# Gate values taken out of the gathered rows, routed rows weighed by token in the attention

## What is computed

```python
xn = layernorm(x)                                  # 8192 x 128
# branch 1: linear attention, 16 heads of 8 channels, in chunks
r, k, v = proj(mix_r(xn)), proj(mix_k(xn)), proj(mix_v(xn))   # mix: xn and xn one token back
A = einsum(r, k) * Wmat                            # inside a chunk
y = A @ v + (r @ state) * wb                       # and from the state before it
state = ws * state + (k * wk).T @ v
s = y @ Wo.T + bo
# branch 2: mixture of experts
probs = softmax(xn @ gate_W.T)                     # 8 experts, the 2 best of each token
routed = sum over the 2 chosen e: probs[e] * (silu(xn @ w1[e]) * (xn @ w3[e])) @ w2[e]
shared = mean over 8 of (silu(xn @ w1s) * (xn @ w3s)) @ w2s
f = 0.5 * shared + 0.5 * routed
out = x + s * silu(f)
```

## Time and profile before

| | us |
|---|---|
| three runs | 879.22, 885.76, 897.25 |
| median | 885.76 |
| the profiled execution | 878.21 |
| its span | 876.4 |

### The profile page before, as it was taken

One profiled execution on the slowest core, in us unless ns is written; L12 is line 12 of the kernel. 1 busy time (PEld: TensorE's weight loads), 2 busy tenths in 40 slices (PEclk: granted clock), 3 DMA queues, 4 the chain that ended last, 5 costly groups with the idle time before them and its releaser, 6 DMA issues.

```text
span 876.4 us, 25917 instructions
## 1 busy us (share of the span) xinstructions
PE 729.4 (83%) x9696; PEld 582.4 (66%) x9696; DVE 585.2 (67%) x1253; ACT 471.9 (54%) x1000; POOL 445.1 (51%) x493
## 2 busy tenths in 40 slices
PE   3777989888788898788879888988889789999993
PEld 2566878766666777667657766766667666676762
DVE  6989988845455755545545455554554489999994
ACT  6755877645454555445545455554555545554551
POOL 2433312346556564555563555545554546666663
PEclk9999999988988989899999999999998899999997
DMA  9921123011111222322222222322232367777641
GB/s 246 227 85 37 41 83 50 14 39 39 38 33 44 78 83 74 112 72 84 77 81 61 87 82 81 114 68 83 82 75 67 110 195 218 214 225 218 194 148 49
DMA packets 106042, 87.83 MB, mean 100 GB/s; under 512 B 20611, under 2 KB 90885, under 8 KB 105925
## 3 DMA queue, kind: packets, MB, share of 16 engines
q1 hardware_dynamic: 96836, 66.96, 26.0%
q0 software_dynamic: 9088, 19.21, 8.6%
HBM read 51.40 MB, written 34.73 MB: 98 GB/s over the span
## 4 chain that ended last, share of the span: by engine, by line
PE 35%; DVE 28%; issue 15%; ACT 10%; another core or an unknown queue 8%; DMA 2%; POOL 1%; ACTq 0%; POOLq 0%; DVEq 0%; SPq 0%
DVE hidden L1099 8%; PE banks L1396 6%; PE banks L1397 5%; PE banks L1398 5%; DVE hidden L1202 4%; DVE wwords L1186 4%; ACT hidden L697 3%; PE banks L1435 3%; PE banks L1414 2%; PE banks L1415 2%; PE banks L1416 2%; PE banks L1530 2%; ACT hidden L702 2%; ACT ybuf L724 2%
## 5 line engine op out<-in xcount | busy, mean ns | idle before, releaser
L1099 DVE TENSOR_TENSOR hidden<-hidden,banks 128x512 f32<-128x512 f32 x206 | 140.7, 683 | 173.9 <-ACT hidden L697 139.7
L576 POOL DMA_INDIRECT srows<-normed_rows,source x142 | 143.9, 1013 | 128.2 <-DVE picked_gate L1080 83.1
L702 ACT CAST hidden<-hidden 128x512 f16<-128x512 f32 x206 | 127.2, 618 | 150.9 <-DVE hidden L1099 135.8
L585 POOL DMA_INDIRECT expert_rows<-ybuf,dest x142 | 144.0, 1014 | 119.7 <-ACT ybuf L724 88.8
L1396 PE MATMUL banks<-sxh,wwords 128*128 128x256 f16 x568 | 164.1, 289 | 27.9 <-issue 21.6
L1397 PE MATMUL banks<-sxl,wwords 128*128 128x256 f16 x568 | 164.3, 289 | 13.0 <-issue 12.8
L1105 DVE TENSOR_TENSOR hidden<-hidden 128x512 f16<-128x512 f32 x178 | 123.1, 692 | 77.3 <-ACT hidden L702 53.0
L1398 PE MATMUL banks<-sxh,wwords 128*128 128x256 f16 x568 | 164.4, 290 | 11.0 <-issue 10.9
L1414 PE MATMUL banks<-wwords,hidden 128*128 (+1 forms) x824 | 155.5, 227 | 12.2 <-issue 6.7
L1416 PE MATMUL banks<-wwords,hidden 128*128 (+1 forms) x824 | 152.7, 226 | 8.9 <-issue 8.9
L1415 PE MATMUL banks<-wwords,hidden 128*128 (+1 forms) x824 | 153.4, 226 | 5.0 <-issue 5.0
(11 more groups left out here) (188 smaller groups left out, 1572.8 us busy)
## 6 DMA issues: line engine op xcount, KB each, us to landing
rows<-x SPq DMA_DIRECT2D x32, 256.0 KB, 4.5
rows<-expert_rows SPq DMA_DIRECT2D x32, 256.0 KB, 3.4
normed_rows<-rows SPq DMA_DIRECT2D x16, 256.0 KB, 5.1
r_rows<-rows SPq DMA_DIRECT2D x32, 128.0 KB
rd_rows<-rows SPq DMA_DIRECT2D x32, 128.0 KB
stage<-r_rows SPq DMA_DIRECT2D x16, 256.0 KB, 4.6
k_rows<-rows SPq DMA_DIRECT2D x32, 128.0 KB
kd_rows<-rows SPq DMA_DIRECT2D x32, 128.0 KB
```

What stands on the lines that cost most here:

```text
L576: G.indirect_dma_start(srows[:, r % NXB, t, :], None, rows_in, bass.IndirectOffsetOnAxis(source[:, r * TPU + t:r * TPU + t + 1], 0)).then_ ...
L585: G.indirect_dma_start(rows_out, bass.IndirectOffsetOnAxis(dest[:, r * TPU + t:r * TPU + t + 1], 0), ybuf[:, r % NYB, t, :], None).then_in ...
L702: A.copy(guh[:, v % 2, h * 2 * UNIT:(h + 1) * 2 * UNIT], gu[:, i % 2, :]).then_inc(sem["gu_hi"], 1)
L1099: V.tensor_tensor(gu[:, i % 2, :], sg[:, i % 2, :], psum[2 * (i % 2) + 1][:, :], ALU.mult).then_inc(sem["gated"], 1)
```

## The change

Gate values no longer travel with the rows. `rows_in` has 128 numbers a row (512 bytes), and the write of the probabilities (`sp_probs`), VectorE's picking of gate values and the expert flags it used are gone. ScalarE copies a routed unit's output unweighted, in one 128x256 operation. The gate value of each token's first and second expert is kept by token: 1/z and exp(second - first)/z, in `zsum` and `pick`, which a second small Exp on ScalarE and a 128x64 product on VectorE make. In the attention ScalarE multiplies the two routed rows of each token by them (`act_weigh`, four 128x128 operations for each of k = 0 and 1) before Pool adds them.

The lists of the attention are put in another order. ScalarE: both weighings of a unit stand around the copy of the state product, and the masks of the next unit are done before the second cast of y. Pool: both additions of a unit stand together, behind the mask of a unit two ahead, and before the last addition of the unit before. SP: the loads of decayed r and k and of the routed rows come ahead of x and of the store.

```diff
-    RW = P + EXPERTS
-    rows_in = nc.dram_tensor("normed_rows", (NTOK, RW), F32, kind="Internal").ap()
+    rows_in = nc.dram_tensor("normed_rows", (NTOK, P), F32, kind="Internal").ap()
...
+        gates = [zsum, pick]
...
-            def sp_probs():
-                nc.sync.wait_ge(sem["gates"], 1)
-                nc.sync.dma_start(rows_in[:, P:RW].rearrange("(t p) e -> p t e", p=P), probs[:, :, :]).then_inc(sem["probs_out"], 16)
...
-            sp_x(0)
-            for u in range(NA + 2):
-                if u >= 2:
-                    sp_end(u - 2)
+            sp_rd(2)
+            for u in range(NA + 1):
+                if u >= 1 and u + 2 < NA:
+                    sp_rd(u + 2)
                 if u + 2 < NA:
                     sp_moe(u + 2)
-                if u + 1 < NA:
-                    sp_x(u + 1)
+                if u + KRING < NA:
+                    sp_kd(u + KRING)
+                if u < NA:
+                    sp_x(u)
+                if u > 0:
+                    sp_end(u - 1)
                 if u + RRING < NA:
                     sp_r(u + RRING)
-                if u + 2 < NA:
-                    sp_rd(u + 2)
                 if u + KRING < NA:
-                    sp_kd(u + KRING)
                     sp_k(u + KRING)
...
             def pool_sorted(r):
...
-                    G.wait_ge(sem["probs_out"], 16)
...
-                    G.wait_ge(sem["gate_picked"], r - NXB + 1)
...
             def pool_add(u, step):
...
-                    G.wait_ge(sem[f"picked{u % PRING}"], 32 * (u // PRING + 1))
+                    G.wait_ge(sem["weighed0"], u + 1)
+                    G.wait_ge(sem["weighed1"], u + 1)
...
             for u in range(-2, NA + 3):
-                if at(u + 1):
-                    pool_add(u + 1, 1)
+                if at(u - 1):
+                    pool_low(2 * (u - 1))
+                    pool_low(2 * (u - 1) + 1)
                 if at(u + 2):
                     pool_mask(2 * (u + 2))
                 if at(u):
-                    pool_end(u)
-                if at(u + 2):
-                    pool_add(u + 2, 0)
-                    pool_mask(2 * (u + 2) + 1)
+                    pool_add(u, 0)
+                    pool_add(u, 1)
+                if at(u - 1):
+                    pool_end(u - 1)
                 if at(u + 1):
-                    pool_low(2 * (u + 1))
-                    pool_low(2 * (u + 1) + 1)
+                    pool_mask(2 * (u + 1) + 1)
...
             def act_route():
-                A.wait_ge(sem["route"], 7)
+                A.wait_ge(sem["route"], ROUTE_CHOSEN)
                 A.activation(ta[:, :, :], ta[:, :, :], ACT.Exp, scale=1.0 / SW).then_inc(sem["exps"], 1)
+                A.activation(top[1][:, :], top[1][:, :], ACT.Exp, scale=1.0 / SW).then_inc(sem["exps"], 1)
...
-                    for t in range(TPU):
-                        i = A.mul(ybuf[:, r % NYB, t, :], src[:, t * P:(t + 1) * P], slot_gate[:, r % GRING, t:t + 1])
-                    i.then_inc(sem["y_out"], 1)
+                    A.copy(ybuf[:, r % NYB, :, :].rearrange("p t d -> p (t d)"), src).then_inc(sem["y_out"], 1)
...
+            def act_weigh(u, k):
+                A.wait_ge(sem[f"picked{u % PRING}"], 32 * (u // PRING + 1))
+                if u == 0:
+                    A.wait_ge(sem["gates"], 2)
+                for b in range(4):
+                    at = tile(u, b)
+                    i = A.mul(picked[k][:, u % PRING, b, :], picked[k][:, u % PRING, b, :], gates[k][:, at:at + 1])
+                i.then_inc(sem[f"weighed{k}"], 1)
...
             for u in range(-2, NA + 3):
-                if at(u):
-                    act_mask(u, 0)
-                    act_mask(u, 1)
-                if at(u - 2):
-                    act_moe(u - 2)
-                    act_high(2 * (u - 2) + 1)
-                if at(u):
-                    act_mask(u, 2)
-                    act_mask(u, 3)
                 if at(u - 1):
-                    act_inter(u - 1)
+                    act_weigh(u - 1, 0)
                 if at(u):
                     act_kv(u, 0)
                     act_kv(u, 1)
                 if at(u - 1):
                     act_high(2 * (u - 1))
+                if at(u + 1):
+                    act_mask(u + 1, 2)
+                    act_mask(u + 1, 3)
+                if at(u - 1):
+                    act_moe(u - 1)
+                if at(u + 1):
+                    act_mask(u + 1, 0)
+                    act_mask(u + 1, 1)
+                if at(u - 1):
+                    act_high(2 * (u - 1) + 1)
+                if at(u):
+                    act_weigh(u, 1)
+                    act_inter(u)
...
-                V.memset(eun[:, :, 0:1], 1.0).then_inc(sem["unit_step"], 1)
...
-                V.tensor_tensor(eun[:, :, 0:EXPERTS - 1], eun[:, :, 0:EXPERTS - 1], eun[:, :, 1:EXPERTS],
-                                ALU.subtract).then_inc(sem["unit_experts"], 1)
...
-                V.tensor_tensor(probs[:, :, :], ta[:, :, :], rep(zsum[:, :], EXPERTS), ALU.mult).then_inc(sem["gates"], 1)
+                V.tensor_tensor(pick[:, :], top[1][:, :], zsum[:, :], ALU.mult).then_inc(sem["gates"], 1)
```

39 lines of the change are left out of this document (8 added, 31 removed).

## The result

The changed kernel took 841.22 us (median of 4 runs, 838.31 to 843.32), beside 885.2 us (879.22 to 897.25) for the kernel before: 0.952 of it, 95% interval 0.946 to 0.958. Its profiled execution took 841.8 us with a span of 840.0 us, 36.4 us less than before. I had forecast 880 us and a range of 862 to 898, so the size was wrong, and with it the forecast of no change that can be measured.

What follows compares the result with a forecast made beforehand. TensorE, losing 136 us beside Pool's indirect transfers, bounds the routed stage; VectorE runs gapless in the attention's middle units. -0.95 - 0.9 = -1.85 us gave 876.4 us profiled, 883.9 on the median's scale; predicted 880, range 862 to 898.

Steps and rivals of the forecast that it cites:

- Gathers: Routed stage: Pool waits only for the transpose, gather starts about 1 us earlier, row 6% shorter; taken as 0.
- the routed stretch moving by over 10 us: Sign, routed stage: the prediction is wrong if the stretch with gathers moves by over 10 us.
- ScalarE in the routed units: Routed stage: one copy for two multiplications saves 0.25 us per unit, hidden from TensorE; 0, bounds 0 and -17 us.
- rival C: Routed stage: shorter eviction shows through Pool's burst, up to 0.25 us per typical unit, -5 to -17 us; chance 0.15.
- Rival B: Routed stage: shorter rows shrink the transfers' drag on TensorE, a quarter -17, all -68 us, 808 to 859; chance 0.08.
- VectorE in the routed units: Routed stage: two small operations leave each unit; at most TensorE's 6.8 us of waits could return; taken as 0.
- Before the routed units: Before the routed stage: flags operation, memset and smaller product gain, small Exp loses 0.2 us; together -0.95 us.
- The 4.80 us pace: Routed stage: a unit without gathers was expected to stay at 4.80 us, near 6.9 us with gathers.
- ScalarE in the attention: Attention: 128 added multiplications at 0.30 us each, 38 us in all, fill holes of 1.53 and 1.32 us; nothing starts later.
- rival A: Attention slips behind ScalarE if four multiplications exceed about 1.6 us: 888 to 896 us on the profiled scale; chance 0.13.
- Start of the attention: First half of the attention: mask no longer behind an addition, VectorE's selection sooner; -0.9 us, bounds 0 and -0.92.
- A unit of over 10 us proves me wrong: Sign, attention: the prediction is wrong if a unit there takes over 10 us; 9.8 us expected.

Runs made afterwards that it cites:

- b_nowait2: Kernel before; VectorE's picking reads only flags and Pool's gather does not wait for it, weighing left out: 853.1 us, 0.969; as b_nowait on chip 7: 742.0 us.
- a_wait: Changed kernel with one added wait, no work: Pool's gather also waits for VectorE's low part of the unit three before: 864.2 us, 0.979 of the kernel before.
- b_512_2: Kernel before with gathered rows of 512 bytes and gate values picked from wrong numbers, all waits kept: 882.5 us, 1.002 of the kernel before.
- a_544_2: Changed kernel with 544-byte rows gathered whole, the last 8 numbers unread: 835.0 us, 0.946 of before; as a_544 on chip 7: 742.8 us, 1.002.
- b_both: Kernel before with one unweighted 128x256 eviction copy and no gather wait for VectorE's picking; 544-byte rows and picking operations stay: 841.2 us, 0.954.
- a_two: Changed kernel with the eviction as two 128x128 multiplications by a column of ones: 847.4 us, 0.957 of the kernel before.
- b_again: Kernel before, unedited, run again on chip 15: 884.2 us, 1.002 of the kernel before.
- a_noweigh: Changed kernel without ScalarE's 128 multiplications of the routed rows, Pool waiting for the loads instead: 839.9 us, 0.950 of the kernel before.
- b_lag6: Kernel before with scatters one unit later and four result buffers instead of three, the wait for VectorE's picking kept: 916.2 us, 1.049.
- a_lag6: Changed kernel with scatters one unit later and four result buffers instead of three: 832.1 us, 0.941 of before; run again: 824.9 us, 0.945.
- a_again: Changed kernel, unedited, run again on chip 15: 837.4 us, 0.947 of the kernel before.
- b_copy: Kernel before with one unweighted 128x256 eviction copy, weighing left out: 743.9 us, 1.001 on chip 7; run again on chip 15: 873.1 us, 0.994.

## Why the prediction was wrong, point by point

**Gathers, the step that failed.** I wrote that Pool would no longer wait for VectorE's reading, that the gather would start about 1 us earlier, that the data are used units later, and took 0. The waits view of POOL before, 180 to 690 us:

```profile
POOL srows L576 <- DVE picked_gate L1080: 83.1, 20, 7.4
```

The runs show 28 us for the wait alone (b_nowait2), 24 to 28 seen from the other side (a_wait). Each half of the step was wrong. "About 1 us" did not come from the row: the 83.1 us of waiting for the picking fell on 20 gathers, so 4 us each. And to ask who waits for the data was the wrong question. The same text held that TensorE loses its time beside Pool's transfers; then when the transfers run matters as much as what they carry, and an edit that moves 83 us of Pool's waiting had to be priced through that. And one of my signs of being wrong, the routed stretch moving by over 10 us, is the one that came. I had put "the unknown" of this edit into the rivals, and no rival was about Pool's wait.

**ScalarE in the routed units, mis-sized.** I took 0 with bounds 0 and -17, because TensorE does not wait for it. The single edit gives -5 us. Beside the edit of the wait it is worth more: 0.969 with the wait gone alone, 0.954 with both, 0.015 x 883 = 13 us. That fits rival C: ScalarE writes, Pool's transfers follow, and typical units shortened by 0.2 to 0.3 us (6.9 to 6.6), as it said. I gave it 0.15. That TensorE's completions are held until the transfers are through, as rival C has it, no run shows: the trace has TensorE's time under "issue" and ScalarE's under "remote", so the wait list has no entry that would name it.

**Rival B, the row's length:** refuted (b_512_2, a_544_2). Rows at a pitch of 544 bytes took Pool 1013 ns and rows of 512 took 1018. I had leant on the Trainium skill for it (DMA: Bandwidth & Descriptors, How a descriptor splits into AXI transactions), which has extra beats for what does not start at a multiple of 256 bytes. For the packets themselves the trace does not speak against it: those of Pool's queue took 134 ns on average in a_544_2 (9.1% of 16 engines over 835.9 us, 9088 packets) and 124 in the changed kernel (8.4% over 840.0 us). The kernel's time does not show it.

**VectorE in the routed units:** 0 was right. b_both keeps the picking operations and has the whole gain (0.954 beside 0.952).

**Before the routed units:** -0.95. From place 6 to place 7 the first Silu gained 0.59 us on the kernel before, as forecast for the expert flags. The rest can't be told: place 23 stands at 172.5 and 172.3 us in two profiles of the kernel before, at 169.0 and 171.3 in two of the changed one. The small Exp took 0.24 us and the small product 0.23, where I had 0.2 for each.

**The 4.80 us pace:** it became 4.48 without gathers, 0.3 less, since the eviction is in that pace too: with two evictions again (a_two) the commonest pace is 4.72. I had expected 4.80 to stay.

**ScalarE in the attention and rival A:** right. The weighing took 20.4/64 = 0.32 us of busy time each, where I had 0.30 and a range of 0.28 to 0.32. By the figures that I took from the Trainium skill (ScalarE: Activation LUTs, What ACT_TABLE_LOAD costs), four in a row are 386 ns and three times 293, which makes 1.27 us, and the trace agrees: 1.27 and 1.28 us. My 1.17 had counted the first one short too. In the changed kernel's middle unit:

```profile
756.58 0.41 ACT L770 CAST wwords<-hidden 128x256 f16<-128x256 f32 x1 [0.36 <-DVE hidden L1186]
756.89 1.27 ACT L778 ACTIVATE rows<-rows,pick 128x128 f32<-128x128 f32 x4
758.07 0.56 ACT L755 COPY hidden<-banks 128x512 f32<-128x512 f32 x1
758.54 1.27 ACT L778 ACTIVATE rows<-rows,zsum 128x128 f32<-128x128 f32 x4
759.95 0.59 ACT L749 COPY wwords<-banks 128x512 f32<-128x512 f32 x1
```

The holes of 1.53 and 1.32 us are filled as laid out, and the undisturbed unit still takes 9.81 us. "A unit of over 10 us proves me wrong" was a bad test: such units are in both kernels (11.10 in the profile before, 11.06 in b_again), and a_noweigh has them as well.

**Start of the attention:** the 0.9 us did not come. ScalarE's first weighing found no rows:

```profile
662.27 1.28 ACT L778 ACTIVATE rows<-rows,pick 128x128 f32<-128x128 f32 x4 [1.14 <-DMA rows<-expert_rows]
663.46 0.56 ACT L755 COPY hidden<-banks 128x512 f32<-128x512 f32 x1
```

and VectorE's selection at 664.12 waited 1.04 us for that copy, where it had waited 0.92 us. I had named this as what would eat the gain. The end is as before, 8.6 us from the last gating to the last instruction.

**TensorE's clock, a term put at nothing:** it is not in my sum, though the earlier trace rows had a granted clock of 0.93 for the stretch. It rose to 0.97. From place 23 to place 99 the time at the lower level is 75 us before and 24 after, and each such microsecond costs at most half of itself, so up to 26 us of the 39 may have passed through it. I read it as a consequence that makes pauses dearer, which no run tests: the clock falls after pauses, as in the row of b_lag6 above, and the longest of them in the kernel before, from 180 us on, is 1.9 us. It follows the time loosely: 123 us at the lower level in b_lag6 and 3 in a_lag6, but 44 in a_again, which is as fast as the profile with 24.

## What to carry to other kernels

Where an engine loses time beside another one's transfers, a wait of the issuing engine is not idle time that costs nothing: ask how it spaces the transfers, and whether a long wait is followed by a long row of them. Put such waits on the earliest event that is true, and read who ended the idle time and how often (83.1 us over 20 gathers), not only whether the data are late. And where a drag of over 100 us has no releaser in the trace, price each edit near it by a range as wide as its share of the drag, since the same kernel can run without the drag elsewhere and the edit is then worth nothing. And where a row shows a granted clock below 1.00, give it a term of its own in the sum.

## What the runs showed of the hardware that I had not expected

- The same kernel takes 743 us on one chip (the median of 31 runs) and 874 to 884 us on three others. Over the routed stretch TensorE's pauses of over 0.3 us are 3 to 4 us in each of b_copy, b_nowait and a_544 on that one, 70 and 76 us in the two profiles of the kernel before on the others; the time at the lower clock level is at most 3.4 us there, 75 and 65 here. Pauses and half of the lower clock make some 100 us of the 137 by which the stretch of the kernel before (501.0 us) is longer than that of b_copy on chip 7 (364.3 us). The rest is not placed.
- Where the drag is, a row of four transfers goes with 0.55 us of pauses, one of six with 2.4, one of eight with 3.3. On chip 7 a row of 268 went with 3.6.
- Pool's own time for a transfer says nothing of it: 1013 ns with the drag, 1053 without. Nor does the packets' time: those of Pool's queue took 133 ns on average in the kernel before (8.6% of 16 engines over 876.4 us, 9088 packets) and 137 in b_copy on chip 7 (10.5% over 741.9 us).
- TensorE's clock fell to its lower level 17 times between 180 and 674 us of the kernel before, where the longest pause of TensorE is 1.9 us.

What in the chips makes the difference stays open; no run here can tell it. So does whether gathers or scatters do it more: neither was left out alone.
